# Attention of an attention and mixture-of-experts block in groups of four heads: turns on VectorE in 32x32 blocks, small fp32 matmul tiles

## The reference

```python
xn = _layernorm(x)
# attention
h = _rmsnorm(xn, norm_scale)
q = einsum('bsd,dhe->bshe', h, wq) * 64 ** -0.5
k = einsum('bsd,dhe->bshe', h, wk)
v = einsum('bsd,dhe->bshe', h, wv)
weights = softmax(einsum('bqhd,bkhd->bhqk', q, k), axis=-1)
new_vals = einsum('bhqk,bkhd->bqhd', weights, v)
attn = einsum('bqhe,hed->bqd', new_vals, w_out) + b_out
# router and experts
logits = silu(xn @ rw1 + rb1) @ rw2 + rb2
k_logits, k_index = top_k(logits, 2)
k_prob = softmax(k_logits)
for e in range(8):
    we = sum(where(k_index == e, k_prob, 0))
    ffn += we * (silu(xn @ w1[e] + b1[e]) @ w2[e] + b2[e])
out = x + attn + ffn
```

## Time and profile before

| | |
|---|---|
| median of 3 runs | 2018.02 us |
| lowest, highest | 2014.84, 2019.52 us |
| profiled execution, its own time | 2015.25 us |
| its span | 2013.4 us |
| granted clock of TensorE, mean | 0.989 |
| busy: TensorE, ScalarE, VectorE, GpSimd | 1946.6, 1574.0, 1538.4, 918.5 us |

### The profile page before, as it was taken

One profiled execution on the slowest core, in us unless ns is written; L12 is line 12 of the kernel. 1 busy time (PEld: TensorE's weight loads), 2 busy tenths in 40 slices (PEclk: granted clock), 3 DMA queues, 4 the chain that ended last, 5 costly groups with the idle time before them and its releaser, 6 DMA issues.

```text
span 2013.4 us, 45217 instructions
## 1 busy us (share of the span) xinstructions
PE 1946.6 (97%) x16646; PEld 1256.0 (62%) x16646; DVE 1538.4 (76%) x2654; ACT 1574.0 (78%) x3716; POOL 918.5 (46%) x790
## 2 busy tenths in 40 slices
PE   7999999999999999998899999999999999999997
PEld 5666656565666656555566666666666666666664
DVE  6888888888888888877677777777777777777775
ACT  6777777777777777775588888888888888888885
POOL 4244455453344344431024646445446455454454
PEclk9999999999999999998899999999999999999999
DMA  2023232211111111110323334333433333343332
GB/s 85 28 62 107 91 101 91 83 67 41 40 40 44 42 41 43 34 38 28 102 68 80 85 85 84 87 81 84 87 80 85 85 80 92 81 84 82 80 75 47
DMA packets 132697, 141.96 MB, mean 71 GB/s; under 512 B 25438, under 2 KB 99038, under 8 KB 132446
## 3 DMA queue, kind: packets, MB, share of 16 engines
...
...
## 4 chain that ended last, share of the span: by engine, by line
PE 78%; ACT 11%; DVE 4%; issue 3%; DMA 2%; another core or an unknown queue 0%; SPq 0%; POOL 0%; POOLq 0%; ACTq 0%; DVEq 0%
PE pair L380 22%; PE pair L348 16%; PE pair L363 11%; PE pair L275 7%; PE pair L277 5%; PE pair L276 5%; ACT PR L1024 4%; PE pair L292 3%; PE pair L399 3%; PE pair L401 3%; PE pair L522 1%; PE pair L523 1%; PE pair L521 1%; DVE NM L646 1%; ACT V L1046 1%
## 5 line engine op out<-in xcount | busy, mean ns | idle before, releaser
L1024 ACT ACTIVATE PR<-pair,NM 128x512 f32<-128x512 f32 x1024 | 717.8, 721 | 19.5 <-DVE NM L646 17.5
L646 DVE TENSOR_REDUCE NM<-pair 128x2 f32<-128x1024 f32 x512 | 611.5, 1211 | 48.1 <-PE pair L348 43.5
L1038 ACT COPY PT<-pair 128x512 f32<-128x512 f32 x640 | 357.8, 607 | 350.7 <-PE pair L363 350.7
L348 PE MATMUL pair<-KS,QS 64*128 64x512 f32 x3072 | 491.1, 423 | 14.9 <-DVE KS L639 10.5
L380 PE MATMUL pair<-PT,V 128*64 128x512 f32 x2048 | 471.7, 603 | 0.2
L363 PEld LDWEIGHTS pair<-idn,PR 64*128 64x128 f32 x8192 | 337.5, 139 | 99.9 <-ACT HS L1072 26.2
L348 PEld LDWEIGHTS pair<-KS,QS 64*128 64x128 f32 x3072 | 257.3, 188 | 176.0 <-issue 129.5
L363 PE MATMUL pair<-idn,PR 64*128 64x64 f32 x8192 | 342.5, 223 | 21.2 <-ACT HS L1072 15.6
L1302 POOL TENSOR_TENSOR HH<-ZZ,HH 128x512 fp32r<-128x512 f32 x156 | 199.2, 1347 | 291.4 <-ACT HH L1123 291.4
L1309 POOL DMA_INDIRECT out<-YS,IDW x156 | 247.0, 1584 | 186.4 <-DVE YS L933 127.9
L380 PEld LDWEIGHTS pair<-PT,V 128*64 128x64 f32 x2048 | 136.5, 137 | 259.4 <-issue 253.5
...
## 6 DMA issues: line engine op xcount, KB each, us to landing
...
RB<-l_rows SPq DMA_DIRECT2D x127, 256.0 KB
...
```

The source lines that it names most:

```text
L348: m = pe.do.matmul(bank[bk + j], a[half[j], cols], c[half[j], :], start=(k == 0), stop=(k == 2))
L646: dve.do.tensor_reduce(NM[:, 2 * t:2 * t + 2], pairs[BANK["S", n, t] // 2][:], AX.X, ALU.max, negate=True).then_inc(sem["dve_max"])
L1024: act.do.activation(PR[:, k, :], bank[BANK["S", n, t] + j], ACT.Exp, bias=NM[:, k:k + 1], accum_out=RS[:, n % 2, j, t:t + 1]).then_inc(sem ...
L1038: act.do.copy(dst[r], src[r]).then_inc(sem["act_PT"])
```

## The change

Attention goes from pairs of heads to groups of four heads (two pairs). `GROUPS` is 64 now, and the loop over G runs over `TIMES` = 256 values and 4 more, four per group g (k = 0 to 3), two steps of scores in each. A step s of a group is 32 queries in each of four column tiles and both heads of the row halves: tile c takes pair c % 2 and query half c // 2.

- Queries and keys are stored once, as fp32, by ScalarE. Scores are 8 fp32 matmuls of 64x32 (rows x columns of the array). There are two pairs of banks for scores; step s waits for the exponentials of s - 2.
- VectorE turns the exponentials in 32x32 blocks, SBUF to SBUF, 1024 elements per partition and step, into PT, a ring of 12 slots. TensorE turns them no more.
- The weighted values are 128 fp32 matmuls of 32x64 per group, 256 columns each: key k of each block of 16 in 32 rows, eight tiles. Half of them stand in k = 0 and half in k = 1 of the next group, and hold the other four banks.
- V goes through DRAM (`v_rows`) to come back in 32-row form, twice: 4 stores per projection, 4 loads per group on SP.
- Those four banks are dealt in turn (`Ring`) to all other work, which stands in k = 2 and k = 3. `project_out` does one group at a time.
- Tiles of experts: parts t0 (y of the tile before, h), t1 (back, rows of the next, y) and t2 (back, h, rows of the next) for every two tiles, each in one of the steps k = 2 and 3. Row additions stand with `back`. Routing parts move by one or two values of G.
- The order lists, `PLAN`'s tables, `TURN_ON`, `VALUES_ON`, `HOLD` and the broadcast of the last pair by TensorE (`spread`) are gone.

The core of the diff:

```diff
-        V = sb("V", [P, QT, H * DH])
-        QS = sb("QS", [P, 2, 2, S], F32R)
-        KS = sb("KS", [P, 2, 2, S], F32R)
-        PR = sb("PR", [P, 8, S])
-        PT = sb("PT", [P, 4, QT, S])
-        NM = sb("NM", [P, 8])
+        VS = sb("VS", [P, 2, 512])
+        V4 = sb("V4", [P, 2, S // 32, 2 * DH])
+        QS = sb("QS", [P, 2, 2, S])
+        KS = sb("KS", [P, 2, 2, S])
+        PR = sb("PR", [P, 2, 2, S])
+        PT = sb("PT", [P, 2, S // 32, 32 * RING])
+        NM = sb("NM", [P, 4, 2])
...
-        RB = sb("RB", [P, 2, S])
-        OT = sb("OT", [P, 4, S])
+        RB = sb("RB", [P, GH, S // 2])
+        OT = sb("OT", [P, GH, S // 2])
...
-        l_rows = nc.dram_tensor("l_rows", (2, 2 * QT, P), F32, kind="Internal").ap()
+        l_rows = nc.dram_tensor("l_rows", (2, GH, 2 * STEPS, 32), F32, kind="Internal").ap()
+        v_rows = nc.dram_tensor("v_rows", (2, GH, 32, S // 32, 2 * DH), F32, kind="Internal").ap()
...
+        def place_of(g, s):
+            slot = (STEPS * g + s) % RING
+            return slot, sorted((STEPS * g + k) % RING for k in range(STEPS)).index(slot)
+
+        def tick(j):
+            return FIRST if j == 0 else FIRST + 3 + (j - 1) // 2 * 4 + (j - 1) % 2
+
+        PLAN = {G: [] for G in range(TIMES + 8)}
+        AHEAD = {G: [] for G in range(TIMES + 8)}
+        PLAN[FIRST - 1].append((0, "turn"))
+        for i in range(0, NT, 2):
+            t0, t1, t2 = (tick(3 * (i // 2) + k) for k in range(3))
+            if i:
+                PLAN[t0].append((i - 1, "y"))
+                PLAN[t1].append((i - 1, "back"))
+            for tile, G in ((i, t0), (i + 1, t2)):
+                if tile < NT:
+                    if tile == i + 1:
+                        PLAN[G].append((i, "back"))
+                    PLAN[G] += [(tile, "h", c) for c in range(NC)]
+                    AHEAD[G + 1] += [(tile, "halves", 3)]
+            if i + 1 < NT:
+                PLAN[t1].append((i + 1, "turn"))
+            PLAN[t1].append((i, "y"))
+            if i + 2 < NT:
+                PLAN[t2].append((i + 2, "turn"))
+        PLAN[TIMES].append((NT - 1, "back"))
 
...
+            def scores(g, s):
+                step = STEPS * g + s
+                at = 32 * place_of(g, s)[1]
+                pe.wait_ge(sem["act_k"], 2 * g + 2)
+                pe.wait_ge(sem["act_q"], 2 * g + 2)
+                pe.wait_ge(sem["act_exp"], 2 * step - 2)
+                for c in range(4):
+                    for r in range(2):
+                        rows = slice(DH * r, DH * r + DH)
+                        cols = slice(c // 2 * 256 + at, c // 2 * 256 + at + 32)
+                        m = pe.do.matmul(bank[2 * (s % 2) + r][32 * c:32 * c + 32, :], QS[rows, g % 2, c % 2, cols],
+                                         KS[rows, g % 2, c % 2, :], start=True, stop=True, tile_position=(DH * r, 32 * c))
                 m.then_inc(sem["pe_S"])
...
+            def weighted(g, half):
+                if half == 0:
+                    pe.wait_ge(sem["dve_tr"], STEPS * g + STEPS)
+                    pe.wait_ge(sem[f"V4_{g % 2}"], 64 * (g // 2 + 1))
+                    for a in range(GH):
+                        came_free(GH + a)
+                for k in range(8 * half, 8 * half + 8):
+                    for c in range(2):
+                        for a in range(GH):
+                            rows = slice(32 * a, 32 * a + 32)
+                            if g % 3 == 1:
+                                moving = PT[rows, c, k, :].rearrange("p (h q) -> p h q", h=3)[:, 0::2, :]
+                            else:
+                                moving = PT[rows, c, k, g % 3 * 64:g % 3 * 64 + 256]
+                            m = pe.do.matmul(bank[GH + a][DH * c:DH * c + DH, 0:256], V4[rows, g % 2, k, DH * c:DH * c + DH], moving,
+                                             start=(k == 0), stop=(k == 15), tile_position=(32 * a, DH * c))
+                if half == 1:
+                    m.then_inc(sem["pe_PV"])
+                    for a in range(GH):
+                        free[GH + a] = sem["dve_OT"], 2 * g + a // 2 + 1
...
+            def project_out(g):
+                bk = ring.take(("OP", g))
+                p = g % 4 * 2
+                pe.wait_ge(sem["dve_OT"], 2 * g + 2)
                 pe.wait_ge(sem["load_wo"], 16)
                 came_free(bk)
...
+                gr, k = divmod(G, 4)
+                if k == 2 and 0 < gr <= GROUPS:
+                    project_out(gr - 1)
+                if k >= 2 or gr == 0:
+                    half, t = divmod(2 * gr + k + 2, 4) if k >= 2 else (0, 2 * k)
+                    for u in (t,) if k >= 2 else (t, t + 1):
+                        if half < 2 * NB:
+                            values(half // 2, half % 2, u)
+                if k >= 2 and gr + 1 < GROUPS:
+                    project(2 * gr + k, True)
+                    project(2 * gr + k, False)
...
+            for G in range(TIMES + 4):
+                g, k = divmod(G, 4)
+                if g < GROUPS:
+                    scores(g, 2 * k)
+                    scores(g, 2 * k + 1)
+                if k < 2 and 0 < g <= GROUPS:
+                    weighted(g - 1, k)
+                attending(G)
+                experts(G)
+                route(G)
+
...
+            def turn_probs(g, s):
+                step = STEPS * g + s
+                slot = place_of(g, s)[0]
+                dve.wait_ge(sem["act_exp"], 2 * step + 2)
+                if step >= RING:
+                    dve.wait_ge(sem["pe_PV"], (step - RING) // STEPS + 1)
+                dve.do.transpose(PT[:].rearrange("p c k q -> p (c k) q")[:, :, 32 * slot:32 * slot + 32],
+                                 PR[:, step % 2].rearrange("p r k -> p (r k)")).then_inc(sem["dve_tr"])
...
+            for G in range(TIMES + 4):
+                g, k = divmod(G, 4)
+                for i, _, c in AHEAD[G]:
+                    halves(i, c)
+                if k == 0 and 0 < g <= GROUPS:
+                    denominators(g - 1)
+                if k == 2 and 0 < g <= GROUPS:
+                    weighted(g - 1)
+                if g < GROUPS:
+                    maxima(g, 2 * k)
+                    maxima(g, 2 * k + 1)
+                if k == 2 and 0 < g <= GROUPS:
+                    project_out(g - 1)
+                if g < GROUPS:
+                    turn_probs(g, 2 * k)
+                attending(G)
+                experts(G)
+                route(G)
+                if g < GROUPS:
+                    turn_probs(g, 2 * k + 1)
 
...
+            def probs(g, s):
+                step = STEPS * g + s
+                act.wait_ge(sem["dve_max"], step + 1)
+                if step >= 2:
+                    act.wait_ge(sem["dve_tr"], step - 1)
...
+            def attending(G):
+                gr, k = divmod(G, 4)
+                if k >= 2 or gr == 0:
+                    half, t = divmod(2 * gr + k + 2, 4) if k >= 2 else (0, 2 * k)
+                    for u in (t,) if k >= 2 else (t, t + 1):
+                        if half < 2 * NB:
+                            values(half, u)
+                if k >= 2 and gr + 1 < GROUPS:
+                    project(2 * gr + k, True)
+                    project(2 * gr + k, False)
 
...
+            for G in range(TIMES + 4):
+                g, k = divmod(G, 4)
+                for i, _, c in AHEAD[G]:
+                    halves(i, c)
+                if g < GROUPS:
+                    probs(g, 2 * k)
+                    probs(g, 2 * k + 1)
+                attending(G)
+                splitting(G)
+                experts(G)
+                route(G)
...
+            def add_rows(i):
+                pool.wait_ge(sem["dve_ys"], i + 1)
+                added_before(("sadd", i))
+                for t in range(QT):
                     pool.do.indirect_dma_start(
                         out, bass.IndirectOffsetOnAxis(ap=IDW[:, i % 4, t, 0:1].bitcast(U32), axis=0), YS[:, i % 2, t, :], None,
                         compute_op=ALU.add).then_inc(sem["sadd"], 16)
...
+            def store_values(half, t):
+                u = 4 * half + t
+                sp.wait_ge(sem["act_V"], u + 1)
+                if half >= 2:
+                    sp.wait_ge(sem[f"V4_{1}"], 64 * (half - 1))
+                dst = v_rows[half % 2][:, :, 4 * t:4 * t + 4]
+                src = VS[:, u % 2].rearrange("p (n e) -> p n e", n=GH)
                 for k in range(4):
...
+                    sp.do.dma_start(dst[:, :, k].rearrange("n i e -> i n e"), src[32 * k:32 * k + 32]).then_inc(sem[f"v_{u % 2}"], 16)
+
+            def load_values(g):
+                half = g // 2
+                for k in range(2):
+                    sp.wait_ge(*side("v", 4 * half + 2 + k, 64))
+                if g >= 2:
+                    sp.wait_ge(sem["pe_PV"], g - 1)
+                for a in range(GH):
```

(1 more changed line is left out.)

706 lines of the change are left out of this document (219 added, 487 removed), and 3 rows, old and new, of the table HOLD.

## The result

The changed kernel takes 2363.8 us (median of 4 runs, 2361.5 to 2366.5), the kernel before 2018.8 in the same comparison (median of 4, 2014.8 to 2020.4): a ratio of 1.171, interval 1.169 to 1.174. It is 345 us slower. The prediction said slower with 0.72 and 2130 us; 2364 also lies above its range, which ended at 2330. The profiled execution took 2362.72 us, its span 2360.9.

The account below looks back on a forecast made before the run. TensorE, busy 97%, bounds the kernel before; without its transposes, the rigid order of VectorE's turns and the expert chain takes over. 2015 + 0 (routing half) + 113 (expert half) = 2128, on the median's footing 2130 us; range 1945 to 2330.

Parts of the forecast that it names:

- two rivals that ended faster: Whole kernel: waits overlap and TensorE's relief shows, 1965 us, chance 0.17; VectorE's turn runs two elements per cycle, 1945, chance 0.08.
- 28.0 us per tile: Expert half: laid-out 27.4 us per tile plus clock loss, against 25.1 before, so +113 us over 39 tiles.
- Routing half: Eight steps of the loop over G laid out from VectorE's queue and waits: 56.15 us against 56.2, no gain.
- the products, the sum and `place`: Routing half, one of eight steps: two products 1.25, sum 0.6 and `place` 2.0 between the turns, 8.45 us.
- plain step: Step with only maxima and turns on VectorE: 5.2 us, TensorE's scores and half of the values fitting beside it.
- TensorE's sum: -236 +31 = about -205 us: TensorE's queue: 8192 transposes gone, -236 us; scores in eight fp32 tiles, +31 us; about -205 if it stayed the bound.
- Sum 109.5 us for three groups: Expert half: three groups with four tiles laid out at 34.6, 39.4 and 34.9 us plus 0.6, 27.4 per tile.
- the second kind: Expert half, group with h in k = 2, y and h in k = 3: second turn at 28.6, 39.4 us in all.
- `halves` of 1.26 each: Expert half, GpSimd: each `halves` after the row additions takes 1.26 us, done at 19.1 us, y waiting for them.
- Four row additions of 1.85: Expert half, GpSimd in the group with y and h in k = 3: four at 1.85 us each, ahead of `halves`.
- Covered: 512 stores and 256 loads of V through DRAM have a group's length, over 20 us, before use, so cost nothing.
- Small tiles do not fill the array: Rival on the values matmuls: 4.5 to 5.5 us per half, 2260 us; four tiles at once, beyond 2500; chance 0.10.

Follow-up runs that it names:

- both turns first: Changed kernel with VectorE making both turns of a step before attending, experts and route: 2294.9 us, in a later set 2302.9 us.
- all four edits: Changed kernel with both turns first, no row scatters, GpSimd low halves of 64 columns after the first tile, plain transfers for indirect row additions: 2137.0, repeated 2135.7 us.
- experiment 5: Changed kernel, ScalarE writing exponentials straight into PT, VectorE turning one block column only: 2227.7 us; its step timeline is read in the kernel without scatters.
- narrow low halves: Changed kernel with GpSimd subtracting only 64 of 512 columns of each low half after the first tile: 2314.2 us.
- plain additions: Changed kernel with the expert half's 156 indirect row additions made plain transfers: 2220.4 us, in a set where the kernel before took 1996.6.

## Why the prediction was right and wrong

**Right: the direction, and a part of the mechanism.** TensorE lost its transposes and waits appeared, in part because the order became rigid: both turns first gave back 69 and 61 us, no turn at all 136. The turn was taken as 1.21 us and took 1.24. VectorE's busy time was put at 1695 and is 1752, ScalarE's at 1250 and is 1307. The projection waits for `OT`, the clock in the expert half is under 0.97:

```profile
100.00:1000.00 900.00, 772.17 (x11465) 408.40 (x11457) 688.94 (x1134) 470.65 (x1186) 355.19 (x338) 0.94 0.40 100
1200.00:2000.00 800.00, 647.53 (x8911) 402.80 (x8912) 579.73 (x608) 470.54 (x1078) 350.46 (x261) 0.92 0.50 108
```

(windows of the changed kernel; the number behind the five engines is the granted clock, 0.94 and 0.92). The two rivals that ended faster fell with the turn's 1.24 us and the tiles' 30.2.

**Near by luck: 28.0 us per tile and 2130 us.** The kernel of all four edits shows 27.7 us per tile and 2135.7 us. But the layout had the second turn behind `halves`, full low halves and indirect additions in it, and that kernel has none of them; its 8 steps take 58.4 and not 56.15. So these two numbers don't bear out the layout. What does compare is the changed kernel itself, with 30.2 us per tile.

**Wrong, by its steps:**

- *"Routing half", "Sum 56.15, against 56.2 now. No gain".* It measured 66.4. The scatters are 6.2 of it (66.4 - 60.2), in 15 rounds 93 us, and the runs gave 89 and 94. No term and no rival had GpSimd's scatters; they were not part of the change, and I only asked what the change adds to each queue, not what the old queues do to a new stream of small matmuls. Without this term the time of 2274.4 or 2269.6 us lies within the range.
- *The remaining 4 us per 8 steps.* The step of the products, the sum and `place`, laid out at 8.45 us from VectorE's work alone, measured 13.1. It left out that TensorE, once let through its gate by the products, has 7.5 us of its own to do before the next scores (experiment 5). The step ahead of it, with `second` and `counts`, was laid out at 7.3 and took 5.6, as a part of its VectorE work falls behind the next scores; the two together took 18.7 us for 15.75, and the other six 1.0 more than laid out. The plain step "5.2 us" is 5.52 and TensorE's: two scores of 0.93 (0.87 taken) and a values half of 3.65 (3.45 taken, 3.7 the upper bound).
- *"TensorE's sum: -236 +31 = about -205 us".* TensorE's busy time is 1946.0 us against 1946.6. The values' matmuls are busy 563.5 us against 471.7, the scores' 552.9 against 491.1. TensorE is busy for 252 us in stretches at the lower clock, 30 us before, so up to half of that, 126 us, is the clock's, an estimate. With all four edits its busy time is 1835.9. The prediction had the clock at 0 to 5 us per three groups of the expert half, up to 1.25 us per tile; there TensorE is busy for 120 us at the lower clock, so the price is up to 1.5 us per tile.
- *The expert half, "Sum 109.5 us for three groups".* The changed kernel takes 122.2. Read between the ends of the second turns (means over nine groups of each kind, in the order in which the prediction lists them), k = 2 and 3 take 24.6, 34.5 and 24.3 us where 23.05, 28.6 and 23.5 were laid out, and k = 0 and 1 behind them 13.7, 11.5 and 13.6 where 10.8, 10.8 and 11.4 were. So most of the miss is in the second kind, where y waits for GpSimd, and in the steps k = 0 behind late low halves. The next two points are the terms in question: with narrow low halves the 34.5 are 30.1 and the 13.6 are 12.1, with plain additions 31.8 and 12.0.
- *"`halves` of 1.26 each".* They took 1.61 in the mean (median 1.74), and beside them 16 of VectorE's 156 additions took up to 4.6 us, 45 us more than at 693 ns in all. The kernel before has 1.35 for them in the mean, and three additions over 1 us: I took both prices from rows in which the two engines rarely meet. Narrow low halves gave back 49.5 us.
- *"Four row additions of 1.85"* stood in one of three groups' chains (the two starts in the earlier trace rows are 1.90 apart). Made cheap, they gave about 50 us, as the low halves behind them come sooner.
- *"Covered", the loads of V.* Right: three runs that moved or removed them changed nothing. No run touched the stores.
- *"Small tiles do not fill the array"* was the rival nearest in time (2260 us) and is not what happened. An undisturbed half takes 3.64 us, 28 ns a record, so its 4.5 to 5.5 us are refuted. By the rule of the Trainium skill, page "TensorE: Matmul & The Clock Gate", section on packing small matmuls, as the prediction read it, the load of each fp32 matmul's second record would have shown; the 3.64 us leave no room for it.

The four edits alone give 69, 89, 49.5 and about 50 us, 257 in sum; together they give 2363.8 - 2135.7 = 228, so they overlap by about 30. Of the 118.6 us that they leave over the kernel before beside them, 63.8 go with the turns and 54.8 stay open, with the clock as one candidate.
